# A graph-attention kernel: the turned one-hots made by ScalarE in two passes instead of by VectorE in one

## The reference

```
xn  = layernorm(x);  xp = xn @ W
alpha = leaky_relu(a_src[src] + a_dst[dst], 0.2)
w   = exp(alpha - amax[dst]);  w /= segment_sum(w, dst)[dst]
x1  = x + elu(segment_sum(xp[src] * w, dst) + bias)
h   = layernorm(x1)
out = x1 + h + where(selected by top-k of h @ wr, ffn(h) * weight, 0)
```

## Time and profile before

| what | before |
|---|---|
| median of three runs | 2208.46 us |
| the profiled execution's span | 2573.5 us |
| first and last start of a gather (L692) | 132.5 us, 2481.3 us |
| PE, DVE, ACT, POOL busy | 1981.2, 1581.4, 744.5, 1554.5 us |
| mean granted TensorE clock | 0.870 |

### The profile page before, as it was taken

The page is one execution under the profiler, slowest core; times in us unless marked ns, Lnnn a source line. Parts: engine busy times, 40 slices in busy tenths (PEclk is TensorE's granted clock), DMA queues, the critical chain, the costliest instruction groups (busy, mean ns, idle before and its releaser), DMA issues.

```text
span 2573.5 us, 29095 instructions
## 1 busy us (share of the span) xinstructions
PE 1981.2 (77%) x9511; PEld 1633.8 (63%) x9512; DVE 1581.4 (61%) x3510; ACT 744.5 (29%) x1478; POOL 1554.5 (60%) x1626
## 2 busy tenths in 40 slices
PE   8935877877877877878778877877777777877787
PEld 6723666666666666666666666666666666666666
DVE  4555655665655655656656665666665665666576
ACT  4512222222322222322232232232232232223223
POOL 2366666666666666666666666666666666666630
PEclk9967988888888889889888888988988988889889
DMA  8844444444444444444444444444444444444447
GB/s 287 276 143 121 123 134 124 132 138 120 137 138 118 132 135 124 135 140 120 134 137 128 130 136 124 134 134 130 128 134 131 127 139 124 131 136 136 119 159 312
DMA packets 157137, 369.12 MB, mean 143 GB/s; under 512 B 46646, under 2 KB 73682, under 8 KB 155699
## 3 DMA queue, kind: packets, MB, share of 16 engines
q0 software_dynamic: 75088, 208.19, 30.1%
q1 hardware_dynamic: 74706, 145.62, 16.9%
q10 hardware_dynamic: 7184, 13.41, 1.4%
HBM read 328.20 MB, written 38.89 MB: 143 GB/s over the span
## 4 chain that ended last, share of the span: by engine, by line
POOL 38%; issue 23%; PE 19%; another core or an unknown queue 9%; DVE 3%; DMA 3%; ACT 2%; POOLq 1%; DVEq 0%; SPq 0%; ACTq 0%
POOL rows L692 38%; PE ag_ps L1057 7%; PE h_ps L1021 4%; PE ag_ps L934 3%; PE y_ps L1040 3%; DMA rows<-node_rows,ends 3%; POOLq L402 1%; DVE oh L1366 1%; DVE rows L1404 1%; ACT hT L808 1%; PE ag_ps L1128 0%; ACT L808 0%; PE ag_ps L1129 0%; ACT L812 0%
## 5 line engine op out<-in xcount | busy, mean ns | idle before, releaser
L692 POOL DMA_INDIRECT rows<-node_rows,ends x1563 | 1512.9, 968 | 850.6 <-issue 482.5
L1057 PE MATMUL ag_ps<-rows,oh 128*128 128x260 f32 x3518 | 845.9, 401 | 47.5 <-DVE rows L1404 34.8
L1021 PE MATMUL h_ps<-xnT,w1s 128*128 128x256 f32 x1568 | 534.0, 500 | 419.2 <-DVE zz L1385 227.1
L1057 PEld LDWEIGHTS ag_ps<-rows,oh 128*128 128x128 f32 x3518 | 716.7, 204 | 180.3 <-DVE rows L1404 37.8
L1021 PEld LDWEIGHTS h_ps<-xnT,w1s 128*128 128x128 f32 x1568 | 377.0, 250 | 517.9 <-DVE zz L1385 234.8
L1404 DVE TENSOR_TENSOR rows<-rows,xl_ps 128x512 f32<-128x512 f32 (+3 forms) x392 | 503.1, 1346 | 47.2 <-issue 26.5
L1385 DVE TENSOR_TENSOR zz<-rows,edge_dm 128x72 f32<-128x72 f32 x98 | 22.9, 233 | 695.0 <-DMA rows<-node_rows,ends 656.4
L1040 PE MATMUL y_ps<-w2s,hT 128*128 128x256 f32 x1568 | 368.0, 386 | 12.2 <-DVE oh L1366 9.2
L831 ACT COPY rows<-rows 128x780 f32<-128x780 f32 x97 | 81.6, 842 | 998.6 <-DMA rows<-node_rows,ends 998.6
L1040 PEld LDWEIGHTS y_ps<-w2s,hT 128*128 128x128 f32 x1568 | 301.7, 194 | 66.7 <-DVE oh L1366 16.6
L1366 DVE TENSOR_TENSOR oh<-xl_ps,dloc 128x2304 f32<-128x2304 f32 x98 | 249.0, 2541 | 0.0
(11 more groups left out here) (243 smaller groups left out, 1433.7 us busy)
## 6 DMA issues: line engine op xcount, KB each, us to landing
dbc<-dst SPq DMA_DIRECT2D x97, 576.0 KB
rows<-node_rows,ends POOLq DMA_INDIRECT x1563
selfr<-node_rows SPq DMA_DIRECT2D x98, 130.0 KB
base<-in_x SPq DMA_DIRECT2D x14, 896.0 KB, 7.1
base<-in_x SPq DMA_DIRECT2D x49, 256.0 KB
ffn_rows<-yb ACTq DMA_DIRECT2D x48, 256.0 KB
node_rows<-base SPq DMA_DIRECT2D x13, 910.0 KB, 5.7
base<-in_x_turned SPq DMA_DIRECT2D x14, 384.0 KB, 7.7
```

The costliest lines, as they stand in the source:

```text
L692: pool.indirect_dma_start(out=rows[:, b, t, :], out_offset=None, in_=table, in_offset=bass.IndirectOffsetOnAxis(ap=ends[:, b, t, 0:1], axi ...
L1021: last = nc.tensor.matmul(h_ps[:, m * PAIR:(m + 1) * PAIR], w1s[:, c, n * P:(n + 1) * P], xnT[:, c, :], start=(c == 0), stop=(c == DC - 1))
L1057: product = nc.tensor.matmul(ag_ps[b][:, 0:ROW], oh[:, b, t, :], rows[:, b, t, :], start=(t == 0), stop=False)
```

## The change

ScalarE makes the turned one-hot: `Square(target - node)` over the tile in place, then `Relu(1 - 2*that)`, each over 128x2304 elements. It makes that of window w+2 in its window w, right after `after_sum` of window w-1 and ahead of `carry` of window w+1; those of the first two windows are made ahead of the loop. VectorE makes only the negative node numbers for it once (`minus_id`, one instruction). TensorE's `look_up` gets one more wait (`dm_ok`), and its last part of `hidden` waits for `dm_ok` (L1373) in place of `oht_ok`. VectorE's minimum with zero becomes a `tensor_tensor` against a column of zeros that is broadcast. The register load of `optional_landed` is now bounded by minimum and maximum instead of an assertion whose check at run time is left out; two loads on branches for extra tiles or the exact maximum change likewise.

```diff
+        minus_id = spare[:, 0:NW]
...
+        def counted_before(eng, w, k):
+
+            return eng.value_load(win[0:1, bass.ds(COLS * w + k, 1)], min_val=0, max_val=NW * EP // P)
+
         def optional_landed(eng, w):
-            landed = eng.value_load(win[0:1, bass.ds(COLS * w + 7, 1)])
-            return nc.s_assert_within(landed, 16, 16 * (NW + 3), skip_runtime_bounds_check_because="a parity's first node block has one gather or more, each later one two at most")
+            return eng.value_load(win[0:1, bass.ds(COLS * w + 7, 1)], min_val=16, max_val=16 * (NW + 3))
...
-                    before = entry(eng, w, 2, NW * EP // P)
+                    before = counted_before(eng, w, 2)
...
+            def one_hots_turned(w, i, b):
+
+                flat = tiles_of(w) * P
+                act.wait_ge(ld_dbc[b], 16 * (i + 1))
+                nc.scalar.activation(oht[:, b, 0:flat], dbc[:, b, 0:flat], ACT.Square, bias=minus_id[:, bass.ds(w, 1)]).then_inc(apart_ok, 1)
+                act.wait_ge(apart_ok, w + 1)
+                nc.scalar.activation(oht[:, b, 0:flat], oht[:, b, 0:flat], ACT.Relu, bias=1.0, scale=-2.0).then_inc(oht_ok, 1)
...
+                if not isinstance(w, int) or w + 2 < NW:
+                    one_hots_turned(w + 2, i + 1, b)
                 exponentials(w + 1, i + b, 1 - b)
...
             nc.scalar.preload_act_table_set(EXP_AND_LN)
+            act.wait_ge(minus_ok, 1)
+            for w in range(2):
+                one_hots_turned(w, 0, w)
             exponentials(0, 0, 0)
...
                 pe.wait_ge(oht_ok, w + 1)
+                if known(w, 1):
+                    pe.wait_ge(dm_ok, w)
...
-                        pe.wait_ge(oht_ok, w + 3)
+                        pe.wait_ge(dm_ok, w + 2)
                     hidden(w - 3, 1 - b, i - 2 + b, (0,))
...
+            nc.vector.tensor_scalar(minus_id, node_id[:, :], -1.0, None, ALU.mult).then_inc(minus_ok, 1)
...
-            def one_hots_turned(w, i, b):
+            def local_targets(w, i, b):
 
                 n = tiles_of(w)
-                flat = n * P
-                dve.wait_ge(ld_dbc[b], 16 * (i + 1))
-                nc.vector.tensor_scalar(oht[:, b, 0:flat], dbc[:, b, 0:flat], node_id[:, bass.ds(w, 1)], None, ALU.is_equal).then_inc(oht_ok, 1)
                 dve.wait_ge(ld_ends[b], 16 * (i + 1))
...
-                nc.vector.tensor_scalar(zmin[:, :], zag[:, :], 0.0, None, ALU.min).then_inc(zmin_ok, 1)
+                nc.vector.tensor_tensor(zmin[:, :], zag[:, :], zero.broadcast_to([P, D]), ALU.min).then_inc(zmin_ok, 1)
...
-                    one_hots_turned(w + 1, i + b, 1 - b)
+                    local_targets(w + 1, i + b, 1 - b)
...
+            then(nc.vector.memset(zero, 0.0))
+            local_targets(0, 0, 0)
```

More of the change, by code:

```diff
@@ L172, in build @@
         xdiff = sb("xdiff", [P, H])
-        column = sb("column", [P, 17])
-        rs1, rstd, sq, half, xloc, broken, broken_all, widest, in_order, first_f, length, nge, cur, kth, sixteen, always, first_block = (column[:, k:k + 1] for k in range(17))
+        column = sb("column", [P, 18])
+        rs1, rstd, sq, half, xloc, broken, broken_all, widest, in_order, first_f, length, nge, cur, kth, sixteen, always, first_block, zero = (column[:, k:k + 1] for k in range(18))
         xmax = sb("xmax", [P, H])
@@ L315, in build @@
          count_ok, before_ok, win_ok, gmax_ok, gall_ok, exact_ok, sdiff_ok, exself_ok, parts_ok,
-         pre) = sems(
+         pre, minus_ok, apart_ok) = sems(
             "pool_const col_ok const_ok ones_bf_ok d16_ok falls_ok earlier_ok blocks_ok block_ok b2_ok bias_step wext_mul_ok wext_ok stat_ok aggr_ok vareps_b rstd_b proj_ld trb_ok trc_ok xp_ok xpc_ok asd_ok "
-            "count_ok before_ok win_ok gmax_ok gall_ok exact_ok sdiff_ok exself_ok parts_ok pre")
+            "count_ok before_ok win_ok gmax_ok gall_ok exact_ok sdiff_ok exself_ok parts_ok pre minus_ok apart_ok")
         ld_ends, ld_dbc, ld_self, gath, gath_last = (sem2(n) for n in ("ld_ends", "ld_dbc", "ld_self", "gath", "gath_last"))
@@ L433, in if_exact @@
                     n = entry(eng, w, 3, EP // P)
-                    before = entry(eng, w, 4, NW * EP // P)
+                    before = counted_before(eng, w, 4)
                     with eng.If(n > 0):
@@ L1512, in _ @@
             then(nc.vector.tensor_copy(iota_ps, iota_d[:, :]))
-            one_hots_turned(0, 0, 0)
+            then(nc.vector.memset(zero, 0.0))
+            local_targets(0, 0, 0)
             one_hots(0, 0)
```

## The result

| | before | after |
|---|---|---|
| median of the runs taken side by side (9 each) | 2210.04 us | 2220.19 us |
| ratio, with its 95% interval | | 1.0039 (1.0027 to 1.0051) |
| span of the profiled execution | 2573.5 us | 2218.4 us |

The change costs 9 to 10 us where 12 were expected to be saved. The profile of before was of one unusual execution: the timed runs of that same kernel have a median span of about 2209 us, and stalls of mostly 2.5 to 3.5 us ahead of gathers, 122 waits for something remote or for ScalarE's carry, hold 358 of its 365 us beyond the median. No later trace has these waits. So the earlier trace rows and the page after can't be subtracted from each other in the idle columns; for these I use the kernel `load_only` of the first experiments (the kernel before with the bounded load alone), which has an ordinary profile.

The account below looks back on a forecast made before the run. GpSimd's gathers were taken to set the pace. Terms -13.7 - 2 + 2 + 1 = -12.7, with minus_id -12.4, took the median of 2208.5 to 2196 us; range 2170 to 2228.

Parts of the forecast that it names:

- Part 1: L1355 leaves VectorE, so GpSimd gathers overlapping it are no longer held: -13.7 us, bounds 0 and -29.7.
- Part 3: TensorE's new gate starts the last part of hidden up to 0.8 us earlier: -2 us.
- part 4: VectorE's two-tensor minimum takes 0.13 us more per window, and TensorE waits for it in 20 windows: +2 us.
- part 5: Bounded load on VectorE's queue ahead of L1385 adds 0.3 us, covered in 83 windows: +1 us, bounds 0 and +29.
- What bounds the kernel: GpSimd's gathers set the pace: 20.2 us a window in timed runs against VectorE's 16.8, margin 3.4.
- rival A: Gathers on GpSimd only wait longer at their gates, so freed time becomes waiting: 2207 us, chance 0.17.
- rival C: TensorE idles longer before the first part of hidden and its clock falls: +30 us, 2239 us, chance 0.08.
- Part 2: Two one-hot passes on ScalarE, 2.09 us each, fit in its idle time before the carry: 0, bounds 0 and +30.
- rival D: ScalarE is late for look_up if a pass takes 3 us: 2225 us, slower, chance 0.06.
- E: VectorE's chain leads, so minimum and load cost in full and the port gives half: 2219 us, chance 0.07.
- F: The remaining small tensor_scalars L1359 and L1360 hold the same gathers just as long: 2211 us, chance 0.07.
- B: Each blocked gather counts in full and TensorE's waits in part, so more is saved: 2177 us, chance 0.15.

Follow-up runs that it names:

- load_onehots: The changed kernel with the old one-input minimum put back, keeping bounded loads and one-hots on ScalarE; 2213.07 us, 1.0008 of before.
- steps_psum: The changed kernel with the residual's running value kept in PSUM, so its steps read at most one SBUF tensor; 2210.26 us, 0.9992 of before.
- load_max: The kernel before with the loaded value's lower bound taken by a maximum in a register, without the run-time assertion; 2213.14 us, 1.0011 of before.

## Why the prediction was wrong

The forecast of 2196 us was for a gain; the result is 2220.19, slower by more than the 0.3% that decide, and inside the range. Three terms of the sum were mis-sized. Parts 1 and 3 were to bring 15.7 us and brought 4 to 6, part 4 was to cost 2 and cost 7 to 9, part 5 was to cost 1 and cost 6. No one of them turns the sign by itself. By its steps:

**What bounds the kernel.** Right in the main: the gathers set the pace, and the span goes with their busy time between kernels that differ by the minimum. It doesn't between those that differ by the one-hots: `load_only` has the longer gathers (1505.5 us against after's 1501.9) and the shorter span. The chain of `load_only` shows that VectorE was less covered than the 3% of the earlier trace rows let it seem; in the kernel after it has 2%.

```profile
POOL 29%; PE 24%; issue 20%; DVE 17%; DMA 7%; ACT 1%; POOLq 1%; DVEq 0%; SPq 0%; ACTq 0%
```

Wrong was the prediction in its reading of the 365 us between span and median. I put them on all windows as the cost of recording. They were one execution's stalls; the spans of later profiles are within 0.6% of the timed medians. The 20.2 us a window that I got for the timed runs was right all the same: after has 20.25 in the median.

**Part 1, -13.7 us: the step that failed by most.** L1355's held gathers did go: 1505.5 to 1493.2 us, which is 12.3, and the mean 963 to 955 as forecast. The 21 us of held gathers in the prediction were those of the unusual execution; in `load_only` L1358 holds them for 12.2. In the profile of before, 36 gathers with 6.6 us had started up to 0.48 us ahead of L1355, so they came first and were held all the same. The rule of the Trainium skill on which the prediction drew ("SBUF — State Buffer", Who interferes with whom), that whoever comes second is blocked, doesn't cover them. What failed more is the price: the prediction put 65% of the gathers' time on the path by the chain's share, but of 12.3 us the time fell by 4 to 6 only. The rest became gaps between the gathers, as rival A had it. Their idle time grows from 496.6 to 506.7 us. What the gaps hold beyond the usual 0.30 us each goes from 6.8 us in `load_only` to 16.4 in `load_onehots` (15.2 in after), most of it in a dozen gaps of 1.0 to 1.6 us. The profile puts most of these down to "issue", so which gate they wait for stays open. TensorE's windows with a first part of hidden above 1.99 us rise from 35 to 57 of 93 (rival C's mechanism, at a price that can't be its 30 us); whether that is behind the gaps wasn't settled.

**Part 2, 0: right.** 2.20 and 2.12 us a pass against 2.09, and ScalarE is not late (rival D is out). The figure of 570 us ahead of the carry was too high, because the 998.6 of the earlier trace rows held the unusual execution's stalls; `load_only` has 802.7, and 802.7 less two passes, 97 x 4.3, is 386 against the 366.1 measured. The warning of the Trainium skill ("ScalarE: Activation LUTs", Rules for kernel authors) about relu on ScalarE had nothing to decide here: a pass takes 2.12 us there, and ScalarE had the time.

**Part 3, -2: part of the above.** The waits of `load_only`, with L1024 as the line of hidden:

```profile
PEld h_ps L1024 <- DVE zz L1388: 206.9, 93, 3.7
...
PEld h_ps L1024 <- DVE dbc L1358: 96.3, 89, 2.3
```

The wait for the one-hot was 96.3 us in 89 windows, not 26.9 in 34, and after the change 21.4 are left. But the wait for the exponents grew from 206.9 to 239.6: of 74.9 us, 32.7 are only waited elsewhere. What the rest brought can't be told apart from part 1.

**Part 4, +2: the mechanism failed.** It measured +7 to +9. I priced the minimum by its own length, 0.13 us, and by who waits for VectorE's chain; its upper bound, 12.7 us, was the whole length on the path, and that it holds the result is luck. The cost is elsewhere: the instructions behind it move by 0.13 us against a beat of 1.25 us, and L1469 then holds a gather some 0.1 us longer in most windows. The Trainium skill has the rule that I left out ("SBUF — State Buffer", Who interferes with whom): an instruction of VectorE with two inputs in SBUF contends with one of GpSimd that reads SBUF. By the earlier trace rows L1447 has this form, and so, by the kernel, have L1452 and L1455; by the earlier trace rows I looked for the port only at L1355. The runs bear the rule out for gathers: `steps_psum` takes the second input away and 10 us with it. The same section tells of a probe in which `tensor_tensor` didn't stall a DMA, and infers the reason from the ports; here L1464, a `tensor_tensor`, runs as the gather of 1225.12 starts, and that gather is 0.13 us longer.

**Part 5, +1: too small.** It measured +6, of which the assertion's part is some 4 (`load_max`). In 98 windows 6 us are 0.06 us each. I had it hidden in 83 of 98 windows, and then doing it early should have brought the 6 us back in full. It didn't in two kernels of three. So the load's length at that place doesn't account for it; whether here, too, it is a shift against the beat was not tried, and it stays open.

**The rivals.** The outcome is nearest to E's 2219 us, but not by E's way, so that is luck: VectorE's chain doesn't lead in the kernel after (it idles 487.2 us for gathers and has 2% of the chain), it holds gathers. A's mechanism is in the runs: 4 to 6 us are left of 12.3, where A had 0.3 of 13.7. F is out, since the gathers that L1355 held are free. B asked for a faster kernel by the full excess and is out.

**The sum, corrected:** +6 for the load, +7 for the minimum, -4 for the one-hots and the gates: 9 us, and 2220.19 - 2210.04 = 10.

## What to carry to other kernels

Where GpSimd's gathers set the pace, list every instruction of VectorE with two inputs in SBUF that can be under way when a gather starts, not only the long one-input ones, and put one input into PSUM where there is room; then count the held gathers again, since a shift of 0.1 us elsewhere can cost or bring as much. When time is taken off the gathers, price it by what the next wait gives back: here 4 to 6 us were left of 12. An edit that lengthens a step by 0.13 us should be priced by what it moves as well as by its length. And before a stall is taken from a profile, its span is to be set against the spans of the timed runs: if they don't agree, the idle columns belong to that one execution.

## What was not expected of the hardware

- A useless copy of 0.28 us on VectorE in every window made the kernel 6 us faster (`shift_before`), and moving operands to PSUM made one kernel 10 us faster and another, whose minimum it also lengthened by 0.13 us, 6 us slower.
- A gather that starts under a VectorE instruction with two inputs in SBUF is held until that ends, less some 0.13 us: 0.07 us over in the mean where 0.2 us of L1469 are left, 0.18 where 0.3 are, 0.23 where 0.4 are. One that starts before it is not held. The fast one-input L1358 is different: it also holds a gather that has started up to 0.48 us ahead of it. That the gather reads its table of ends from SBUF at its start would fit, but no row shows the read.
- The bounded load's assertion is two instructions of 183 and 23 ns on VectorE's queue, and its 98 windows cost some 4 us, with intervals that overlap.
